# Two-layer attention, FFN and mixture of experts on one core: later routing, a denser scatter, biases moved into the expert steps

## The reference, cut to what matters

```
def fp4_quant_dequant(x):
    xb = x.reshape(..., n // 16, 16)
    scale = max(max(abs(xb)) / 6.0, 1e-12)
    idx = searchsorted(_MID, abs(xb / scale))
    return _GRID[idx] * sign(xb) * scale
...
xn = _layernorm(x)
x = x + _L0_attn_ref(xn, ...) + _L0_ffn_ref(xn, ...)
xn = _layernorm(x)
scores = softmax(xn @ Wg);  top_w, top_idx = top_k(scores, 2);  top_w = softmax(top_w)
combine = sum(one_hot(top_idx) * top_w)
hdn = gelu(xn W1[e] + b1[e]);  y_e = hdn W2[e] + b2[e]
x = x + _L1_attn_ref(xn, ...) + sum_e combine[e] * y_e
```

## Time and profile before

| | |
|---|---|
| median of 3 runs | 1206.04 us (1205.69 to 1212.28) |
| profiled execution | 1211.18 us, its span 1208.9 us |
| busy share of the span | PE 78%, DVE 70%, ACT 50%, POOL 30% |
| chain that ended last | PE 41%, DVE 22%, issue 7%, ACT 6%, unknown queue 4% |
| TensorE's granted clock, mean | 0.929 |

### The profile page before, as it was taken

One profiled execution on the slowest core, in us unless ns is written; L12 is line 12 of the kernel. 1 busy time (PEld: TensorE's weight loads), 2 busy tenths in 40 slices (PEclk: granted clock), 3 DMA queues, 4 the chain that ended last, 5 costly groups with the idle time before them and its releaser, 6 DMA issues.

```text
span 1208.9 us, 35271 instructions
## 1 busy us (share of the span) xinstructions
PE 937.5 (78%) x15195; PEld 508.9 (42%) x15195; DVE 851.6 (70%) x1434; ACT 604.6 (50%) x754; POOL 357.7 (30%) x421
## 2 busy tenths in 40 slices
PE   0577777778888887776787878776698988889887
PEld 0355553334444444343343334433444545455443
DVE  6789947577888888788878756455456576476726
ACT  3223221456655655553445455444356655666566
POOL 3333342203213213213030353542142423423230
PEclk9999976799989999998889889889899999999999
DMA  9600051354243244143221132034245265354217
GB/s 145 230 18 18 27 120 50 68 127 100 54 99 99 55 99 112 45 102 84 48 63 38 46 110 60 25 106 99 67 141 145 78 160 134 106 126 111 60 34 205
DMA packets 115597, 109.31 MB, mean 90 GB/s; under 512 B 13745, under 2 KB 108210, under 8 KB 115058
## 3 DMA queue, kind: packets, MB, share of 16 engines
q1 hardware_dynamic: 108370, 95.30, 31.6%
q0 software_dynamic: 7072, 11.76, 3.7%
HBM read 65.28 MB, written 48.51 MB: 94 GB/s over the span
## 4 chain that ended last, share of the span: by engine, by line
PE 41%; DVE 22%; issue 7%; ACT 6%; another core or an unknown queue 4%; SPq 2%; DMA 2%; POOL 1%; ACTq 0%; DVEq 0%; POOLq 0%
DVE a_maxes L1442 12%; PE a_psO L1225 12%; PE a_psS L1204 5%; PE a_psS L1181 5%; PE a_psS L1066 4%; ACT a_Pt L1290 4%; PE a_psM L1158 2%; PE a_psM L1164 2%; PE a_psM L1243 1%; PE a_psM L1092 1%; DVE xn L1477 1%; PE a_psS L1057 1%; DVE a_ON L1538 1%; PE a_psM L1153 1%
## 5 line engine op out<-in xcount | busy, mean ns | idle before, releaser
L1442 DVE TENSOR_REDUCE a_maxes<-a_psS 128x2 f32<-128x1024 f32 (+3 forms) x432 | 506.3, 1183 | 223.4 <-PE a_psS L1066 120.2
L1290 ACT ACTIVATE a_Pt<-a_psS 128x1024 f32<-128x1024 f32 (+1 forms) x432 | 418.2, 991 | 263.6 <-PE a_psS L1066 166.2
L1225 PE MATMUL a_psO<-a_Pt,V 128*32 128x512 f32 (+3 forms) x2048 | 234.3, 549 | 2.4 <-ACT a_Pt L1290 2.4
L1181 PE MATMUL a_psS<-K,Q 60*64 60x512 bf16 (+3 forms) x2048 | 183.0, 364 | 62.9 <-ACT a_Pt L1290 38.1
L1204 PE MATMUL a_psS<-Q,K 63*64 63x512 bf16 (+3 forms) x2048 | 183.8, 366 | 47.8 <-DVE a_maxes L1442 36.9
L1066 PE MATMUL a_psS<-dist,alpha_eye 64*64 64x128 bf16 x5120 | 170.3, 222 | 7.4 <-issue 7.4
L1066 PEld LDWEIGHTS a_psS<-dist,alpha_eye 64*64 64x64 bf16 x5120 | 140.8, 111 | 65.8 <-issue 18.5
L309 POOL TENSOR_TENSOR qkf<-qkf,parts 128x512 f32<-128x512 f32 x32 | 37.0, 1157 | 339.7 <-ACT parts L1267 337.6
L1204 PEld LDWEIGHTS a_psS<-Q,K 63*64 63x64 bf16 x2048 | 59.2, 106 | 170.3 <-DVE a_maxes L1442 78.2
L1181 PEld LDWEIGHTS a_psS<-K,Q 60*64 60x64 bf16 x2048 | 61.8, 111 | 113.2 <-ACT a_Pt L1290 58.4
L1581 POOL DMA_INDIRECT y<-spare,r_sent_id x64 | 61.6, 962 | 125.0 <-ACT spare L1321 56.4
(11 more groups left out here) (233 smaller groups left out, 1247.9 us busy)
## 6 DMA issues: line engine op xcount, KB each, us to landing
stack<-parts SPq DMA_DIRECT2D x192, 128.0 KB
expert_w<-in_expert_w SPq DMA_DIRECT2D x96, 128.5 KB
Q<-stack SPq DMA_DIRECT2D x64, 192.0 KB
K<-stack SPq DMA_DIRECT2D x64, 192.0 KB
xs<-in_c_no_token SPq DMA_DIRECT2D x24, 258.0 KB, 5.7
slots_flat<-xs SPq DMA_DIRECT2D x24, 258.0 KB
xnT<-xnT_dram SPq DMA_DIRECT2D x16, 256.0 KB, 3.1
slots_flat<-y SPq DMA_DIRECT2D x16, 256.0 KB, 4.8
```

Of the source, the lines that this page charges most:

```text
L1181: pe.matmul(banks[HEAD_ROWS * hf:HEAD_ROWS * (hf + 1), b, x * w:(x + 1) * w], Q[rows, k % 4, q, at:at + HEAD_ROWS], K[rows, k % 4, q, 0:w] ...
L1225: m = pe.matmul(psO[32 * j:32 * (j + 1), q0:T], V[:, (k - 2) // 2 % 2, kt, r, j, :], Pt[:, (nB.at(k) + unit) % RING, h % 2, x // 2 * w:(x ...
L1290: act.activation(Pt[:, u % RING, :, 0:w], psS[:, place_of["B", u] % BANK_PAIRS, :, 0:w], ACT.Exp).then_inc(p_ready, 1)
L1442: dve.tensor_reduce(maxes[:, k % 2, i, :, heads[0] // 2:heads[0] // 2 + pairs], src, AX, ALU.max, negate=True).then_inc(a_free, 1)
```

## The change

- Routing of the sequences 6 and 7: LS to LG in steps 17 and 19 (before 16 and 18), R0 to R3 in 17 and 19 as now but at later slots, R4 to R7 and RN in 18 and 20 (before 17 and 19). LS waits for the WO of the even step before.
- F and TE in step 21 at slots 3, 4, 6, 8 (before step 19, slots 12 to 15).
- Scatter in steps 22 and 23, two transfers per slot (before 20 to 23, one per slot).
- CT and CB in the odd expert steps 25, 27, 29, 31, two sequences each, at slots 0, 1, 10, 11 (before steps 21 and 22); the copy of CT is DVE's, before ACT's.
- SP loads the first expert weights at the end of step 22; at the end of step 23 it waits only for the scatter.
- FFN: the scale is made by a scalar_tensor_tensor with a tensor of constants (`least`) instead of a tensor_scalar; x is added by four products with the identity on PE, and ACT copies the sum to x (before: DVE's `s10`).

```
@@ -45,7 +45,8 @@
-SCATTER_STEPS = range(LAYER_HALVES + 4, LAYER_HALVES + 8)
+SCATTER_STEPS = range(LAYER_HALVES + 6, LAYER_HALVES + 8)
+SCATTERS = 2
@@ -133,8 +134,9 @@
-            at[k] += [(6, ("LS", b)), (7, ("LT", b)), (8, ("RS", b)), (10, ("LN", b)), (11, ("XT", b)), (13, ("LG", b))]
-            at[k + 1] += [(s, ("R%d" % j, b)) for j, s in enumerate((3, 4, 5, 6, 7, 8, 11, 12))] + [(10, ("RN", b))]
+            at[k + 1] += [(s, (what, b)) for s, what in ((1, "LS"), (2, "LT"), (3, "RS"), (6, "LN"), (7, "XT"), (9, "LG"),
+                                                         (10, "R0"), (11, "R1"), (12, "R2"), (13, "R3"))]
+            at[k + 2] += [(s, (what, b)) for s, what in ((2, "R4"), (3, "R5"), (6, "RN"), (7, "R6"), (10, "R7"))]
@@ -162,12 +164,11 @@
-    if k == LAYER_HALVES + 3:
-        side += [(12, ("F", 0)), (13, ("TE", 0)), (14, ("F", 1)), (15, ("F", 2))]
-    if k in SCATTER_STEPS[1:3]:
-        first = 4 * (k - SCATTER_STEPS[1])
-        at = range(4, 12) if k % 2 else (4, 6, 10, 11, 12, 13, 14, 15)
-        side += list(zip(at, [(what, b) for b in range(first, first + 4) for what in ("CT", "CB")]))
+    if k == LAYER_HALVES + 5:
+        side += [(3, ("F", 0)), (4, ("TE", 0)), (6, ("F", 1)), (8, ("F", 2))]
+    if k in EXPERT_STEPS[1::2]:
+        first = k - EXPERT_STEPS[1]
+        side += list(zip((0, 1, 10, 11), [(what, b) for b in (first, first + 1) for what in ("CT", "CB")]))
@@ -320,11 +321,11 @@
-def quant_scales(dve, v, am, sc, rs, sem, base):
+def quant_scales(dve, v, am, sc, rs, least, sem, base):
...
-    dve.tensor_scalar(sc, am, float(np.float32(1.0 / 6.0)) * UP, float(np.float32(1e-12)) * UP, ALU.mult, ALU.max).then_inc(sem, 1)
+    dve.scalar_tensor_tensor(sc, am, float(np.float32(1.0 / 6.0)) * UP, least, ALU.mult, ALU.max).then_inc(sem, 1)
@@ -380,6 +381,7 @@
+        least = n.sb("f_least", [P, HW // BLK], ctx=c)
@@ -414,6 +416,7 @@
+        least_set = n.sem("least_set", c)
@@ -513,7 +516,7 @@
-                                 buf[w + "rs"][:], S[w + "_grid"], QUANT_STEPS * b)
+                                 buf[w + "rs"][:], least[:, 0:buf[w + "sc"].shape[1]], S[w + "_grid"], QUANT_STEPS * b)
@@ -544,26 +547,23 @@
-                def s10(b, p):
-                    dve.wait_ge(S["down"], b + 1)
-                    xv = n.x[:, b * NT:(b + 1) * NT, :]
-                    dve.tensor_tensor(xv, ps_d[:], xv, ALU.add).then_inc(S["added"], 1)
-
...
+                dve.memset(least[:], float(np.float32(1e-12)) * UP).then_inc(least_set, 1)
...
+                dve.wait_ge(least_set, 1)
...
-                quant_scales(dve, blocks(w), w_am, w_sc, w_rs, w_gridded, 0)
+                quant_scales(dve, blocks(w), w_am, w_sc, w_rs, least[:, 0:W // BLK], w_gridded, 0)
...
-                run_ffn_steps([(0, sh), (1, sm), (-1, s10), (2, sx), (1, sm_rest)])
+                run_ffn_steps([(0, sh), (1, sm), (2, sx), (1, sm_rest)])
@@ -592,6 +592,10 @@
+                def add(b, p):
+                    act.wait_ge(S["down"], b + 1)
+                    act.activation(n.x[:, b * NT:(b + 1) * NT, :], ps_d[:], ACT.Copy).then_inc(S["added"], 1)
+
@@ -600,9 +604,10 @@
-                def project(it, which):
-                    if it != SEQS - 2 or which > 2:
+                def project(it, at):
+                    if it != SEQS - 2 or at not in (0, 2, 3):
...
+                    which = (0, 2, 3).index(at)
@@ -631,7 +636,7 @@
-                run_ffn_steps([(1, a5), (1, a5_rest), (0, a10), (2, a1_rest)], project)
+                run_ffn_steps([(1, a5), (-1, add), (1, a5_rest), (0, a10), (2, a1_rest)], project)
@@ -744,8 +749,9 @@
-                            m = pe.matmul(ps_d[:, i, :], hqT[0:r, q, i * P:(i + 1) * P], wdT[0:r, q, :],
-                                          start=(q == 0), stop=(q == FFC - 1))
+                            pe.matmul(ps_d[:, i, :], hqT[0:r, q, i * P:(i + 1) * P], wdT[0:r, q, :],
+                                      start=(q == 0), stop=False)
+                        m = pe.matmul(ps_d[:, i, :], n.ident[:], n.x[:, b * NT + i, :], start=False, stop=True)
@@ -1024,10 +1030,10 @@
-                    if k == EXPERT_STEPS[0] - 1:
+                    if k == EXPERT_STEPS[0] - 2:
...
-                        sp.wait_ge(misc_free, find_misc(SCATTER_STEPS[2], ("CB", SEQS - 1)) + 1)
+                    if k == EXPERT_STEPS[0] - 1:
@@ -1309,8 +1315,6 @@
-                            act.wait_ge(misc_ready, misc_index(k, pos) + 1)
-                            act.activation(ct[0:E], psM[0:E, :], ACT.Copy).then_inc(misc_free, 1)
@@ -1448,7 +1452,7 @@
-                            dve.wait_ge(misc_free, find_misc(k, ("WO", 0)) + 1)
+                            dve.wait_ge(misc_free, find_misc(k - k % 2, ("WO", 0)) + 1)
@@ -1495,8 +1499,10 @@
+                        elif what == "CT":
+                            dve.wait_ge(misc_ready, misc_index(k, pos) + 1)
+                            dve.tensor_copy(ct[0:E], psM[0:E, :]).then_inc(misc_free, 1)
...
-
@@ -1615,15 +1621,16 @@
-                            index = len(units[1][0]) * (k - SCATTER_STEPS[0]) + arg
-                            if index % TILES == 0:
-                                pool.wait_ge(xn_copied, SEQS)
-                                if index:
-                                    pool.wait_ge(placed, 16 * TILES)
-                                set_ids(index // TILES)
-                                pool.wait_ge(slots_ready, index // TILES + 1)
-                            pool.wait_ge(a_free, nA.at(k) + arg)
-                            scatter(index)
+                            for index in range(SCATTERS * arg, SCATTERS * (arg + 1)):
+                                index += SCATTERS * len(units[1][0]) * (k - SCATTER_STEPS[0])
+                                if index % TILES == 0:
+                                    pool.wait_ge(xn_copied, SEQS)
+                                    if index:
+                                        pool.wait_ge(placed, 16 * TILES)
+                                    set_ids(index // TILES)
+                                    pool.wait_ge(slots_ready, index // TILES + 1)
+                                pool.wait_ge(a_free, nA.at(k) + arg)
+                                scatter(index)
```

## The result

The changed kernel takes 1229.73 us (median of 4 runs, 1227.75 to 1235.44) where the kernel before takes 1205.87 (4 runs): ratio 1.021, 95% interval 1.017 to 1.025. It is slower. The profiled execution took 1228.7 us, its span is 1226.3, against 1211.2 and 1208.9.

What follows compares the result with a forecast made beforehand. No single engine: the bound changes by stage, DVE pacing some steps and PE held in others. FFN -2.5, routing -2, scatter +6, second biases +3.5, expert loads -8 sum to -3 on 1206.0: 1203 us, range 1184 to 1228.

Steps and rivals of the forecast that it cites:

- Scatter: Steps 20 to 23: 64 transfers cost 47.5 us before and 53.6 in steps 22 and 23 after, +6 us (-10 to +32).
- The clean lengths: Scatter steps without transfers: 24.0 us for an odd step, 29.7 for an even one, 107.4 for steps 20 to 23.
- the 7 us for the biases beside the scatter: Steps 21 and 22 before the change: the second biases were taken to cost some 7 us there.
- the lower end: Double scatter: 5.1 us for two slots, POOL's own time; the forecast took 6.1, with 7.7 as upper mean.
- The rival at 1187: Steps 22 and 23: holds don't grow with density, the steps take 91 us, total 1187 us; chance 0.27.
- Second biases: Moved from steps 21 and 22 to odd expert steps: cost 10.4 us there, +3.5 us net (0 to +8).
- FFN: Before the attention loop: addition off DVE gains 4.2 us, last sequence loses 1.7, scale form nothing; -2.5 us (-7 to +1).
- the other end: FFN: if the new scale form escapes POOL, 0.9 us less a period; total 1199 to 1200 us, chance 0.08.
- Routing: Steps 16 to 20, last two sequences: moving normalisation and rank steps gives -2 us (-7 to +4).
- First expert loads: Step 24: weights issued a step earlier let the slots' rows load sooner, -8 us (-10 to -4).
- The rival of merged bursts: Steps 22 and 23: bursts merge and hold PE almost throughout, 7.7 us for two slots, total 1229 us; chance 0.18.

Runs made afterwards that it cites:

- e16: Kernel before with each of its 64 indirect scatter transfers replaced by a plain transfer to consecutive rows: 1168.9 us, ratio 0.970 to the kernel before.
- e6: Changed kernel with each of the 64 indirect scatter transfers replaced by a plain transfer to consecutive rows: 1175.6 us, ratio 0.977 to the kernel before.
- e7: Kernel before with the second biases moved to steps 25, 27, 29, 31 and no wait for them before the expert loads: 1214.8 us, ratio 1.011.
- e1: Kernel before with only the scatter moved to steps 22 and 23, two transfers per slot: 1166.8 us, ratio 1.018, on a chip without holds.
- e3: Kernel before with the two FFN edits alone: 1146.5 us, ratio 1.000, on a chip without holds.
- e9: Changed kernel with the second scatter transfer of a slot issued behind the exp: 1178.1 us, ratio 1.028 to the kernel before, on a chip without holds.
- e4: Kernel before with only the first expert weights loaded a step earlier, at the end of step 22: 1136.6 us, ratio 0.991, chip without holds.
- e14: Changed kernel with F and TE in step 20, scatter over steps 21 to 23, second biases in 22 and 23: 1195.5 us, ratio 0.992 to the kernel before.

## Why the prediction was wrong

It said 1203 us, -3, and got 1229.7, +24 by the medians and +17.5 by the profiled executions. Of the 20 us between -3 and the traces, the odd expert steps are 12.8, steps 22 and 23 are 9.0 and steps 16 to 21 are 6.5; the expert loads (-3.7) and the steps without an edit (-5.8) went the other way. By its own steps:

- **Scatter, the step that failed first.** It is the sentence "Steps 20 to 23 took 161.9, clean 107.4 ...: the 64 transfers cost 47.5 us". By e16 the four steps take 127.5 us without holds, so the transfers cost 34.4, and by e6 those of the changed kernel 55.3, where 53.6 stood in the ledger. The cost after was sized well and the cost before 13 us too high, so that a growth of 21 us looked like 6. Two inputs made the 13. The clean lengths came from an estimate of 3.0 us for two slots and from step 18 less its routing: 24.0 and 29.7, where e16's step 23 takes 26.0 and e6's step 22 takes 31.3. And the 7 us for the biases beside the scatter came from no row; e7, without them, is 16 us shorter in steps 21 and 22. The clean lengths are also why steps 22 and 23 were forecast at 107: their clean length was taken as 53.7, and e6 measures 61.0. Of the two reasons given for a value near the lower end, one didn't hold here: the splits were counted as free stretches, but they are what makes the long run, since the slots freed behind them pile up. That the transfers hold the reports, that their price is counted in time, and that on this chip placing ends with step 23, was right (POOL's last transfer ends at 839.3, step 24 begins at 840.0), though PE's own products are held up as well. The rival at 1187 was not to be had on either kind of chip: with no hold at all the same density came back as 19 us in step 24 (e1).
- **Second biases.** "I take 1.0 and 1.6: 4 x 2.6 = 10.4": measured +23.2 (e7: 22.6). The 1.3 (the mean of the two) is less than PE's own work for a bias, 1.16 and 0.6 in the prediction's own terms and 3.5 for two in the traces, in steps in which PE is busy for all but 2.4 us (e3). With the waits over the single buffer psM a bias costs 2.0 us at the full clock (e9), not 1.3, and 2.9 on the mean in the result, at granted clocks of 0.88 to 0.94. The fall of the clock was weighed for the scatter and left out here. What they leave behind in steps 21 and 22 was undersized too, 7 us where e7 gave back 16, and so part of the miss cancels: net +3.5 was forecast, and e7 measures +6.6 in those steps of the trace and +13 (7 to 20 by its interval) in the medians.
- **FFN.** -2.5 forecast, no gain in the period (15.74 for 15.70) and none clear of noise in e3. The value failed, not the bound: 0.9 less a period was named as the other end. The row chosen as the nearest, 1.16 us for an operation with two SBUF inputs beside POOL, gave the new scale's 1.22 nearly to the point; I costed it at nothing since the old form waits for POOL also, but that one ended at 0.61. Where no POOL operation lies beside it, the new form takes 0.19. The Trainium skill's rule (SBUF — State Buffer, "Who interferes with whom"), that a DVE instruction with two SBUF inputs contends with a GpSimd instruction that reads SBUF, agrees with the 1.22.
- **Routing** was right for steps 16, 18 and 20 within 1 us; step 17 was forecast 2.6 too short and step 21 2. In step 17 DVE is busy for 27.3 us before and after, PE 2.0 longer; why it is longer was not tried. Step 21 takes 33.8 in e6, so its 2 us go with the indirect form of the first transfers.
- **First expert loads** were right in kind, and 3.7 us better (e4 -10.9, result -11.7): the rows are issued at 842.29 and PE's slot 4 waits no more.
- **No edit, steps 0 to 15**, -5.8 in the result. These steps are the same in every run, and their length in the other traces stands between +0.3 (e7) and -8.2 us (e14) from that of the kernel before, so the -5.8 is no effect of the change. The traces differ by 17.5 and the medians by 24 because the profiled execution of before was 5.3 above its median and that of the changed kernel 1.1 below.
- **The rival of merged bursts** gave 1229 and was closest, half by accident: the long run is real in step 22, but two slots took (116.3 - 9.7)/16 = 6.66 us on the mean, short of its 7.7 and of the 6.9 from which it was to decide, and with e6's 61.0 as the clean length only 6.2, the forecast's own value; the biases made up the rest. That its number was hit is luck.

The Trainium skill's same section says that PE and ACT never wait on anyone. On chips without holds the traces agree, with no remote wait at all; on those with, ACT's 14.27 us and PE's slow products stand against it, if it is read as a rule for any wait. The section is on the ports of SBUF, and whether these are the path is not known.

## What to carry to other kernels

Before making an engine's side work denser, add its own time (64 x 1.27 us) to what its queue already does in those steps and compare with their length: if it doesn't fit, the work is late or arrives in runs, and in-order work ahead of it (here the splits) decides how long these are. Before moving small work into another step, compare its own time with what the busiest engine has to spare there: two biases are 3.5 us of PE's time, and step 25 had 2.4 to spare. Work is cheap where the engine waits anyway. Take a change apart before judging it: here the early loads were a gain (-0.9%), the FFN edits cancelled each other, the dense scatter and the moved biases were losses (+1.8% and +1.1%), and a milder version of the whole was 0.8% faster than the kernel before. The routing moves were never run alone but for one sequence.
